# One core, attention with max search ahead: 64x32 matmul tiles in the steps, value sums in two key halves, another order inside a step

## The reference, cut to what matters

```python
q, k, v = (proj(w_q), proj(w_k), proj(w_v))          # (2, 32, 1024, 16)
scores = jnp.einsum('bhqd,bhkd->bhqk', q, k) / jnp.sqrt(jnp.float32(D_K))
attn = jax.nn.softmax(scores, axis=-1)
out = jnp.einsum('bhqk,bhkd->bhqd', attn, v)
...
x = x + _L0_attn_ref(_layernorm(x, axis=-1), ...)
x = x + _L0_ffn_ref(_layernorm(x, axis=-1), ...)
```

## Time and profile before

| | |
|---|---|
| median of 3 runs | 962.65 us (962.37 to 963.83) |
| the profiled execution's own time | 963.78 us |
| its span, first to last instruction | 962.0 us |
| granted TensorE clock, mean | 0.987 of full speed |
| busy: PE, DVE, ACT, POOL | 93%, 88%, 78%, 24% of the span |
| chain that ended last | PE 46%, DVE 31%, ACT 10% |

### The profile page before, as it was taken

How to read it: one execution, slowest core, us unless ns; L and a number is a source line. 1 busy time by engine, 2 the same in 40 slices (tenths; PEclk the granted TensorE clock), 3 DMA queues, 4 the chain that set the end, 5 groups by cost and what they waited for, 6 DMA issues and landing times.

```text
span 962.0 us, 17694 instructions
## 1 busy us (share of the span) xinstructions
PE 894.6 (93%) x6232; PEld 294.7 (31%) x6232; DVE 847.1 (88%) x1576; ACT 750.3 (78%) x1468; POOL 233.8 (24%) x367
## 2 busy tenths in 40 slices
PE   4799999999999999999999999999999998999986
PEld 3333222222222222222222222222222224454442
DVE  6877799999999999999999999999999667788975
ACT  4422499888888898899888888888888976777784
POOL 3600011162111111821363431421043222000000
PEclk9989899999999999999999999999999998999999
DMA  8340021121114122331413223141231202111000
GB/s 308 88 161 2 1 54 42 40 56 41 40 34 125 51 88 56 97 100 34 107 45 87 60 81 85 27 113 48 78 122 35 57 20 73 65 46 45 22 34 33
DMA packets 40573, 64.96 MB, mean 68 GB/s; under 512 B 5926, under 2 KB 20774, under 8 KB 40486
## 3 DMA queue, kind: packets, MB, share of 16 engines
q1 hardware_dynamic: 40486, 63.85, 23.2%
HBM read 42.27 MB, written 21.23 MB: 66 GB/s over the span
## 4 chain that ended last, share of the span: by engine, by line
PE 46%; DVE 31%; ACT 10%; issue 6%; DMA 3%; SPq 2%; POOL 1%; ACTq 0%; DVEq 0%; POOLq 0%
DVE mx L1008 22%; PE ps L490 16%; PE ps L410 12%; PE ps L469 8%; ACT PB L775 5%; PE ps L326 5%; DVE XV L1105 2%; PE ps L606 2%; PE ps L635 1%; PE ps L570 1%; ACT XV L845 1%; DMA tu<-wkT 1%; DVE hm L1114 1%; ACT XV L840 1%; ACT PB L856 1%
## 5 line engine op out<-in xcount | busy, mean ns | idle before, releaser
L1008 DVE TENSOR_REDUCE mx<-ps 128x1 f32<-128x512 f32 x1024 | 636.6, 683 | 44.4 <-PE ps L410 42.3
L775 ACT ACTIVATE PB<-ps 128x512 f32<-128x512 f32 x1024 | 537.4, 606 | 77.5 <-PE ps L469 76.3
L410 PE MATMUL ps<-QK 48*128 48x512 f16 x1024 | 334.9, 384 | 27.9 <-DVE mx L1008 23.5
L469 PE MATMUL ps<-QK 50*128 50x512 f16 x1024 | 314.1, 385 | 4.0 <-ACT PB L775 1.4
L490 PE MATMUL ps<-PB,Vg 128*32 128x512 f32 x2048 | 273.3, 606 | 0.0
L410 PEld LDWEIGHTS ps<-QK 48*128 48x128 f16 x1024 | 89.2, 94 | 309.2 <-DVE mx L1008 232.0
L388 PE MATMUL ps<-XV,wqk 64*128 64x512 f16 x624 | 160.6, 377 | 0.0
L469 PEld LDWEIGHTS ps<-QK 50*128 50x128 f16 x1024 | 76.4, 94 | 109.0 <-ACT PB L775 84.8
L1272 POOL TENSOR_SCALAR nmb<-nm 128x16 f16<-128x16 f32 x32 | 6.5, 203 | 366.8 <-DVE nm L1013 366.5
L845 ACT ACTIVATE XV<-XV,magic,hm 128x512 f32<-128x512 f32 (+1 forms) x48 | 33.5, 760 | 40.0 <-DVE hm L1130 40.0
L490 PEld LDWEIGHTS ps<-PB,Vg 128*32 128x32 f32 x2048 | 40.7, 108 | 66.2 <-issue 44.8
(11 more groups left out here) (164 smaller groups left out, 787.2 us busy)
## 6 DMA issues: line engine op xcount, KB each, us to landing
parts_d<-spl SPq DMA_DIRECT2D x64, 128.0 KB
att_d<-OS SPq DMA_DIRECT2D x32, 256.0 KB
XV<-x SPq DMA_DIRECT2D x28, 256.0 KB, 5.3
QK<-parts_d SPq DMA_DIRECT2D x48, 128.0 KB, 2.6
QK<-parts_d SPq DMA_DIRECT2D x16, 256.0 KB, 4.2
XV<-att_d SPq DMA_DIRECT2D x8, 512.0 KB, 3.4
XV<-rden_d SPq DMA_DIRECT2D x8, 512.0 KB, 4.7
out<-PB SPq DMA_DIRECT2D x16, 256.0 KB, 2.0
```

What stands on the lines that cost most here:

```text
L410: nc.tensor.matmul(ps[:, at % S_BANKS, :], QK[rows, sup % 2, 2 * set_ + p, 0, half * HALF + qt * P:half * HALF + (qt + 1) * P], QK[rows, s ...
L469: nc.tensor.matmul(ps[:, T_BANK + t_slot(n) % T_BANKS, :], QK[rows, sup % 2, 2 * set_ + p, 1, kt * P:(kt + 1) * P], QK[rows, sup % 2, 2 * ...
L775: nc.scalar.activation(PB[:, at % 3, 2 * (i // 2) + t_side(step, i), :], ps[:, T_BANK + t_slot(n) % T_BANKS, :], ACT.Exp, scale=exp_reg).t ...
L1008: nc.vector.tensor_reduce(mx[:, v % 2, idx, kh:kh + 1], ps[:, at % S_BANKS, :], AX.X, ALU.max).then_inc(s_used, 1)
```

## The change

Items, transposed scores and pieces, each one matmul of 64x128 (rows x columns of the array) before, become four matmuls of 64x32 that write 32 output partitions each; the value sums, four matmuls of 128x32, become eight of 64x32: four over the keys of one side, and later in the step four over the other side, which wait for the first four (`av_half`). The order in a step is new: all transposed scores stand between the two halves of the value sums, the pieces at the end. `SCORE_SIDES` and `t_side` are changed with it. The last two units keep the wide forms, but for their pieces.

```diff
-SCORE_SIDES = ((0, 0, 0, 0), (1, 0, 0, 1), (1, 0, 0, 1), (1, 1, 1, 1), (0, 0, 0, 0), (1, 1, 1, 1), (0, 0, 0, 0), (1, 1, 1, 1))
+SCORE_SIDES = ((0, 0, 0, 0), (1, 1, 1, 0), (0, 0, 0, 1), (1, 1, 1, 1), (0, 0, 0, 0), (1, 1, 1, 1), (0, 0, 0, 0), (1, 1, 1, 1))
...
-            last = nc.tensor.matmul(ps[:, job_bank(n), :], stationary, moving, start=first_piece, stop=last_piece)
+            for c in range(STRIPS):
+                strip = slice(c * STRIP, c * STRIP + STRIP)
+                last = nc.tensor.matmul(ps[strip, job_bank(n), :], stationary[:, strip], moving, start=first_piece, stop=last_piece)
...
-            return SIDES[i] if step % KEYT in (1, 2, 3, 5, 7) else 1 - SIDES[i]
+            return SIDES[i] if step % 2 else 1 - SIDES[i]
...
+            width = P // strips
+            for c in range(0, P, width):
+                last = nc.tensor.matmul(ps[c:c + width, T_BANK + t_slot(n) % T_BANKS, :],
+                                        QK[rows, sup % 2, 2 * set_ + p, 1, kt * P + c:kt * P + c + width],
+                                        QK[rows, sup % 2, 2 * set_ + p, 0, half * HALF:(half + 1) * HALF],
+                                        start=True, stop=True)
+            last.then_inc(st_psum, 1)
...
+            second = side != first_side(step)
+            if second:
+                pe.wait_ge(av_half, sup * STEPS + step + 1)
+            rows = slice(side * SIDE, side * SIDE + SIDE)
             for h in range(GH):
+                last = nc.tensor.matmul(ps[32 * h:32 * h + 32, av_bank(at), :], Vg[rows, set_, kt, h, :],
+                                        PB[rows, (sup * STEPS + step) % 3, h, :], start=(kt == 0 and not second),
+                                        stop=(kt == KEYT - 1 and second))
+            last.then_inc(av_done if second else av_half, 1)
...
+                    first = first_side(step)
                     item(step, 0)
+                    pe_scoresT(pe, sup, step, 0, STRIPS)
+                    lagging(step, first)
+                    pe_scoresT(pe, sup, step, 1, STRIPS)
                     item(step, 1)
+                    pe_scoresT(pe, sup, step, 2, STRIPS)
                     item(step, 2)
+                    pe_scoresT(pe, sup, step, 3, STRIPS)
                     item(step, 3)
+                    lagging(step, 1 - first)
+                    if r not in (1, 2):
+                        for j in range(4):
+                            piece(j)
```

More of the change, by code:

```diff
@@ L44 @@
 HALF_RANGE = 32768.0
+STRIP = 32
+STRIPS = P // STRIP
 EXPONENT = 0x7F800000
@@ L392, in pe_job_half, with pe_scores @@
                 last.then_inc(job_turn, 1)
-        def pe_scores(pe, sup, unit, k):
+        def pe_scores(pe, sup, unit, k, strips):
             qt, p, side, kh = item_of(sup * 4 + unit, k)
@@ L409, in pe_scores @@
             rows = slice(side * SIDE, side * SIDE + ROWS)
[L410 to L413, removed]
+            width = P // strips
+            for c in range(0, P, width):
+                last = nc.tensor.matmul(ps[c:c + width, at % S_BANKS, :],
+                                        QK[rows, sup % 2, 2 * set_ + p, 0, half * HALF + qt * P + c:half * HALF + qt * P + c + width],
+                                        QK[rows, sup % 2, 2 * set_ + p, 1, kh * HALF:(kh + 1) * HALF],
+                                        start=True, stop=True)
+            last.then_inc(s_psum, 1)
         def t_side(step, i):
-            return SIDES[i] if step % KEYT in (1, 2, 3, 5, 7) else 1 - SIDES[i]
+            return SIDES[i] if step % 2 else 1 - SIDES[i]
         def t_slot(n):
@@ L454, in pe_max_rows, with pe_scoresT @@
             last.then_inc(rows_psum, 1)
-        def pe_scoresT(pe, sup, step, i):
+        def pe_scoresT(pe, sup, step, i, strips):
             unit, kt = step // KEYT, step % KEYT
@@ L468, in pe_scoresT, with first_side, pe_av @@
             rows = slice(side * SIDE, side * SIDE + AUG)
[L469 to L474, removed]
+            width = P // strips
+            for c in range(0, P, width):
+                last = nc.tensor.matmul(ps[c:c + width, T_BANK + t_slot(n) % T_BANKS, :],
+                                        QK[rows, sup % 2, 2 * set_ + p, 1, kt * P + c:kt * P + c + width],
+                                        QK[rows, sup % 2, 2 * set_ + p, 0, half * HALF:(half + 1) * HALF],
+                                        start=True, stop=True)
+            last.then_inc(st_psum, 1)
+        def first_side(step):
+            return 1 - step % 2
+        def pe_av(pe, sup, step, side):
             unit, kt = step // KEYT, step % KEYT
@@ L479, in pe_av @@
             pe.wait_ge(probs, sup * 4 * STEPS + (4 * step + 4))
-            if kt == 0:
+            if kt == 0 and side in (None, first_side(step)):
                 if unit % 2 == 0:
@@ L488, in pe_av @@
                     pe.wait_ge(rows_used, 1)
+            if side is None:
+                for h in range(GH):
+                    last = nc.tensor.matmul(ps[32 * h:32 * h + 32, av_bank(at), :], Vg[:, set_, kt, h, :],
+                                            PB[:, (sup * STEPS + step) % 3, h, :], start=(kt == 0), stop=(kt == KEYT - 1))
+                last.then_inc(av_done, 1)
+                return
+            second = side != first_side(step)
+            if second:
+                pe.wait_ge(av_half, sup * STEPS + step + 1)
+            rows = slice(side * SIDE, side * SIDE + SIDE)
             for h in range(GH):
-                last = nc.tensor.matmul(ps[32 * h:32 * h + 32, av_bank(at), :], Vg[:, set_, kt, h, :],
-                                        PB[:, (sup * STEPS + step) % 3, h, :], start=(kt == 0), stop=(kt == KEYT - 1))
-            last.then_inc(av_done, 1)
+                last = nc.tensor.matmul(ps[32 * h:32 * h + 32, av_bank(at), :], Vg[rows, set_, kt, h, :],
+                                        PB[rows, (sup * STEPS + step) % 3, h, :], start=(kt == 0 and not second),
+                                        stop=(kt == KEYT - 1 and second))
+            last.then_inc(av_done if second else av_half, 1)
         def pe_superunit(pe, sup, last):
@@ L498, in item, with lagging @@
                 if not (last and ahead):
-                    pe_scores(pe, sup + ahead, unit, k)
+                    pe_scores(pe, sup + ahead, unit, k, STRIPS)
+            def lagging(step, side):
+                if step > 1:
+                    pe_av(pe, sup, step - 2, side)
+                elif sup > 0:
+                    pe_av(pe, sup - 1, STEPS - 2 + step, side)
             for step in range(STEPS):
@@ L513, in pe_superunit @@
                     s = step - 2 * KEYT
-                    pe_scoresT(pe, sup, step, 0)
-                    pe_scoresT(pe, sup, step, 1)
+                    pe_scoresT(pe, sup, step, 0, 1)
+                    pe_scoresT(pe, sup, step, 1, 1)
                     for j in range(4):
@@ L521, in pe_superunit @@
                         pe_xq_transpose(pe, (s - 4) // 2)
[L522 to L524 removed]
+                    pe_scoresT(pe, sup, step, 2, 1)
+                    pe_scoresT(pe, sup, step, 3, 1)
+                    lagging(step, None)
+                else:
+                    first = first_side(step)
                     item(step, 0)
[L526 removed]
+                    pe_scoresT(pe, sup, step, 0, STRIPS)
+                    lagging(step, first)
+                    pe_scoresT(pe, sup, step, 1, STRIPS)
                     item(step, 1)
+                    pe_scoresT(pe, sup, step, 2, STRIPS)
                     item(step, 2)
[L529 removed]
+                    pe_scoresT(pe, sup, step, 3, STRIPS)
                     item(step, 3)
[L531 to L549, removed]
+                    lagging(step, 1 - first)
+                    if r not in (1, 2):
+                        for j in range(4):
+                            piece(j)
             if last:
[L551 to L552 removed]
+                pe_av(pe, sup, STEPS - 2, None)
+                pe_av(pe, sup, STEPS - 1, None)
         def out_bank(t):
```

3 lines of the change are left out of this document (2 added, 1 removed).

## The result

The changed kernel takes 982.54 us (median of 4 runs, 981.65 to 986.63) against 962.93 us before: ratio 1.0211, 95% interval 1.0181 to 1.0241. It is 19.6 us slower; 940 was forecast.

A forecast was written before the change was run, and what follows sets the result against it. PE and DVE were taken to run in lockstep, with DVE becoming the bound. Gains of 22 x 0.85 + 8 x 0.55 = 23.1 us off 963.8 gave 940.7, and the median 1.1 lower 940 us; likeliest range 925 to 950.

The forecast's parts named there:

- What bounds the kernel: Attention units: PE and DVE in lockstep; DVE alone takes 0.60 us per maximum, so 1.42 us per unit is waiting.
- The floor of 19.3 us per unit: DVE alone in one attention unit: 32 maxima at 0.60 us plus one small reduction, against 20.72 us taken.
- Shape changes: Around PE's value sums: some 0.2 us per step lost to changing tile shape goes when all use 64x32 tiles.
- Does the other side run meanwhile: PE array: four slots of scores and items, 0.88 us, run on one side beside the first half on the other.
- Order within a step: From last item to next item 0: 0.88 us instead of 1.32, closing 0.30 us gaps at r = 2 and 3.
- The first rival: PE matmuls start strictly in program order: +3 us on 30 units, about 1055 us; chance 0.08.
- the bracket of 965 to 1000: Slower strips in PE: groups 0.08 us later each make a step 2.68 us, about 1000 us; chance 0.10.
- Four instructions for one: PE's fourfold loads and matmuls: 0.45 us issuing per step, hidden; group spread costs 0.18 us per unit.
- rival 2: PE's instruction stream too slow: at 0.056 us per load-matmul pair a unit takes 27 us, about 1150 us; chance 0.09.
- At r = 5: Step with full-array row transposes: last item to next item 0 stays 1.5 us, so 0.29 us of waits are kept.
- The sum: Attention: 0.85 us gained per ordinary unit, 22 x 0.85 + 8 x 0.55 = 23.1 us in all.

The follow-up runs named there:

- half_after_item1: Changed kernel with the first half of the value sums moved behind transposed score 1 and item 1; 951.65 us, ratio 0.9888.
- late_wide: Order of half_after_item1, with items, transposed scores and pieces as one 64x128 matmul each again, value-sum halves still 64x32; 2184.08 us, ratio 2.269.
- strips_only: Kernel before, its order and whole value sums kept, with only items, transposed scores and pieces made of four 64x32 strips each; 970.73 us, ratio 1.0082.
- searched_order: Changed kernel's instructions reordered: item 1 and transposed score 1 ahead of the first half, one piece ahead of item 3; 947.02 us, ratio 0.9846.
- searched_den_later: searched_order plus the output weights' load spread over four units, with DVE's reciprocal of the softmax sums at r = 7 instead of 6; 936.64 us, ratio 0.9725.
- the order and the spread load: searched_order with the output weights' four transfers issued one at a time in units 9, 11, 12 and 15 instead of together; 945.23 us, ratio 0.9836.
- one_head_first: Changed kernel with the first half of the value sums made for only one head of four; 973.34 us, ratio 1.0110.

## Why the prediction was wrong

**What bounds the kernel: right.** DVE alone was reckoned at 0.60 us per maximum; half_after_item1 runs twenty in 12.34 us, 0.61 each, and the next twelve at 0.60. The floor of 19.3 us per unit was a little low, since the twelve in a row are 0.62 apart; the best plain unit measured is 19.78 us.

**Shape changes: right.** The changed kernel has no extra time around the value sums, and late_wide, where the shapes alternate, has no score beside them.

**Does the other side run meanwhile: right about the starts, and it is here that the argument went wrong.** The rows showed starts only the earlier trace rows, and the forecast went from "it starts" to "it is seen 0.43 us after its start". **The step that failed** is the one under *Order within a step*: DVE "needs 0.43 us from an item's start to its own". That held in the kernel before, where nothing long stood ahead of an item and beside it. Behind a first half it is the end of the half that counts. Item 1 started 0.57 us after item 0 (261.14 to 261.71) and was taken 0.95 us after its start (262.66), where 0.43 had been reckoned. The first rival was built from the rule of the Trainium skill, TensorE: Matmul & The Clock Gate, Part 3 (What overlaps and what doesn't), that matmuls start and end in the order of the code. The trace contradicts the part on starts (303.19 ahead of 303.37, and T1 at 261.49 ahead of the half's second pass at 261.87). The part on ends agrees with these runs as far as reports go (none of 238 seen ahead of the half's end). The forecast dropped the whole rule because its part on starts had failed, and that is how the late report was overlooked.

**The side that loses.** The loss came out through item 1 (DVE, gaps of 0.20 to 0.45 us) and T1 (ACT), not through any rival as priced. Rival 1 had strict starts at +3 us a unit. What came was late reports: 21.35 against the 19.97 of half_after_item1, 1.38 us in a plain unit, which turned a gain of 0.75 into a loss of 0.63. The time fell into the bracket of 965 to 1000, to which 0.10 was given for slower strips; that it did so for another reason is chance.

**Four instructions for one: right in a plain unit, too low over the kernel.** 0.18 us per unit was forecast for their spread, and 0.19 was measured (strips_only). The other 3 us of strips_only lie in three units and were in no term. The stream of instructions, held to be hidden, was hidden in plain units; half_after_item1 has one stall of 1.90 us with nothing awaited, next to full DMA engines. The even spacing that rival 2 feared does not show.

**At r = 5:** 0.29 us were kept; half_after_item1 shows 0.21 as idle time there, the same as the earlier trace rows.

**The sum:** 0.85 us per plain unit was forecast; with the reports out of the way it was 0.75 (half_after_item1, 20.72 - 19.97) and 0.94 (searched_order). So the forecast's unit is right for an order in which nothing that is needed early stands behind a half, and that order wasn't the one of the change. The whole sum did not come even then: half_after_item1 gained 10.2 us, not 23.1, since units 11, 17, 21, 25 and 26 got longer by 5.3 us together, most of it in 17 and 21 by the stall and the reciprocal's wait above. Only with the reciprocal moved was it passed (25.9 us, searched_den_later).

## What to carry to other kernels

When matmuls in different tiles of the array pass each other, look at when their consumers start, not at when they do: what is needed soon goes ahead of the long matmul in the code, even if the array could run it beside. A split into many small matmuls multiplies the instruction stream, here from 49 packets to 127; look for stalls with nothing awaited next to large transfers, though moving one such transfer gained nothing measurable here. After speeding up the bound engine, list its waits again: here moving a reciprocal by one step took 8.6 us off, half as much as the order and the spread load had gained over the kernel before (17.3).

## What the runs showed of the hardware that was not expected

- Matmuls of the other row half and of other column strips start ahead of earlier ones, but are reported in the order of the code: T1 ended by 261.90 and was taken at 262.60, the half ahead of it ended at 262.49; with a single strip in the half (one_head_first) the same, 257.80 and 257.89. Whether the results too are complete only then, or only the semaphores wait, these runs don't tell.
- Four 64x32 fp16 matmuls on one side follow each other at 0.22 us like one of 64x128, with the other side busy (261.49 to 261.71).
- PE's weight loads stood still for 1.90 us with nothing awaited, after 1 MB of transfers had filled the DMA engines (share 1.01) and no instruction packet had come for 8.5 us. That the one caused the other is supported, not shown.
- With 64x128 and 64x32 tiles in turn, no score ran beside a value sum, and the granted clock stayed at 0.50 for all of attention.
